# Keys rotated by relative position, context sums beside the query projection, and the two batches' softmax taken apart, in a six-part perceiver kernel

## The chip, the cores and the metric

One Trainium2 chip, one of its cores. The metric is the device time of one execution in microseconds, from the kernel's runs on the chip; the kernel before has a median of 547.14 us over 3 runs.

## What is computed

x (2 x 128 x 256) goes through six residual parts, each behind a layer norm: cross-attention with compressed keys, a state-space layer, a feed-forward, a second cross-attention with quantised operands, an attention over the batch axis, and a gated feed-forward. The change lies in the first one. Its core, in the reference:

```python
kv_c = kv @ W_kvc                       # 2 x 2048 x 64
q_c = q @ W_dq                          # 2 x 128 x 96
q_rope = _rope(q_rope, lq)              # position of the query, 64 columns a head
k_rope = _rope(kv_c @ W_kr, lk)         # position of the key, shared by the heads
scores = (q_nope @ k_nope + q_rope @ k_rope) * scale      # einsum, 16 heads
good = (k_ids <= qs) & (k_ids >= qs - 8)                  # qs: a segment id for each query
scores = jnp.where(good[:, None, :, :], scores, NEG)
out = softmax(scores) @ v                                 # then @ W_o
```

A query sees at most nine keys, those from its segment id less 8 up to the id. If it sees none, softmax over equal values gives the mean of all 2048 values of its batch. The kernel takes that case along as a tenth kind of key, for which it needs the mean of the context over its rows.

## The kernel before

The program is written out by hand for each engine, with counting semaphores between them; each engine works through its list in order, so a wait holds back whatever stands behind it. TensorE's results go to eight PSUM banks of 128 x 512 words (`ps`).

First part, in the order of TensorE's list:

- L1342, L1344: the key up-projection is folded into the query's (`w_qall`, 64 latent and 64 rotated columns a head), and W_kr into `w_kcat`. Then the layer norm's transposes (L1335) and the projection to 96 latents (L1351).
- The query loop, over 8 pairs of heads: L1375 gives 128 rows for each head, 64 latent and 64 to be rotated, for 256 queries; L1377 gives the 64 rotated rows once more with their halves exchanged (`w_qrs`, made by ACT at L714). ACT copies the latent rows to `qT` (L738), DVE multiplies the rows of L1375 by cosines and those of L1377 by sines (L1010, L1012), GpSimd adds both into `qT` (L601). Each output has two banks. From the fourth pair on, `window_columns(0, f)` (L1363, ACT L732) transposes the gathered context rows of batch 0 in between, five groups.
- The nine context rows of each query and nine rows of a table of cosines and sines (`rope`, by the key's position) come by GpSimd's indirect loads (L589, L592), at indices that DVE works out (L974 to L979).
- Keys: L1395 projects the gathered rows with `w_kcat`, three steps a batch, with `window_columns(1, f)` between the batches. ACT copies 64 latent columns to `krow` (L750); DVE rotates the other 64 (L1025 to L1030). SP stores the latents of each batch to DRAM (L506) and, when both are there, loads them back grouped by eight queries in nine loads (L510) to `kvg`, where they serve as values.
- L1404 transposes `krow` to `kcat` in six steps, with ACT L755. L1438 makes the scores, 32 groups of eight queries times 16 heads against 72 keys, four groups a step, and DVE adds the mask (L1034). Both batches' scores stand together, with the products of W_uv and W_o (`weights_vo`, L1413) between.
- Softmax for each batch: maximum (L1045), subtraction (L1046), exponential on ACT (L759), sum (L1039 or L1054), reciprocal (L1040 or L1055), product (L1056).
- Context sums: SP loads the context in eight chunks of 512 rows through two buffers (L494), GpSimd adds four chunks a batch into `csums` of 128 x 4 x 256 (L612), and TensorE sums over partitions and the four tiles with a column of ones (`mean_column`, L1422, 16 matmul records a batch). The mean goes through `w_kcat` (L1453) to `kvm`, copied by ACT for batch 0 (L775) and DVE for batch 1 (L1059), and by a small load (L516) to row 73 of `kvg`.
- L1462 transposes the probabilities in eight steps (ACT L778), L1474 multiplies them with `kvg` in four (DVE L1063 to `oT`), L1479 gives the output, both batches in one bank, DVE adds it to the residual (L1066), and `normalise(1)` follows (L956 to L966).

SP's list before: chunks 0 and 1 (once the rotation rows are there), w0b (W_uv and W_o), chunk 2, store of batch 0, chunk 3, chunk 4, store of batch 1, chunk 5, the nine loads, chunks 6 and 7, w1 (the next part's weights), the small load. GpSimd's list: the gathers, eight additions of the query loop, then the chunks.

An fp32 matmul leaves two matmul records in the trace (a transpose one), so a pair of heads in the loop shows four of L1375 and four of L1377.

## Time and profile before

| | |
|---|---|
| median of 3 runs (lowest, highest) | 547.14 us (542.32, 548.55) |
| the profiled execution | 546.76 us |
| its span, first to last instruction | 544.9 us |
| TensorE matmuls busy | 437.3 us (80%) |
| DVE busy | 398.5 us (73%) |
| ACT busy | 296.0 us (54%) |
| GpSimd busy | 138.8 us (25%) |
| chain that ended last | PE 54%, DVE 17%, issue 14%, ACT 8%, DMA 3% |

The busy shares are means over parts with different limits: the second cross-attention, from about 230 to 480 us, is full on TensorE, DVE and ACT, while the first part has DVE at about a half. So the shares say little of the changed part, and the views of its own stretch are what count. The chain of waits is followed back from the last instruction; in time order it shows at each moment whose work set the end.

### The profile page before, as it was taken

Reading aid. Unit: us, or ns where it says so; the run is one execution under the profiler, and the core shown is the slowest. Engines: PE = TensorE matmul, PEld = TensorE weight load, DVE = VectorE, ACT = ScalarE, POOL = GpSimd, SP = SyncE. Lnnn points to the kernel's source line nnn. Section 1 sums busy time; section 2 is a strip of 40 time slices with the busy share of each in tenths; the row PEclk is TensorE's granted clock in tenths of the full one; section 3 lists DMA queues with packets and bytes.
Section 4 is the critical chain, followed back from the end, with each engine's and each line's share of the span. In section 5 each row is a group of like instructions: output and inputs, shape, how many; then the busy total and the mean of one; then the engine's idle time right before and its main releaser. Section 6 shows DMA issues by size and latency. Waiting matters only on the chain.

```text
span 544.9 us, 9508 instructions
## 1 busy us (share of the span) xinstructions
PE 437.3 (80%) x3874; PEld 328.4 (60%) x3914; DVE 398.5 (73%) x607; ACT 296.0 (54%) x384; POOL 138.8 (25%) x176
## 2 busy tenths in 40 slices
PE   3999887788488777767866789899898988876597
PEld 3556776666265555533753567677677767654486
DVE  6134585357969999995669899999999999613242
ACT  2123424045454444431437899999999999931110
POOL 4124441013545555550001233242111111100000
PEclk9999996989699999989889799999999999977789
DMA  8820692131122111004519545544455334000000
GB/s 300 344 91 0 195 246 100 37 158 36 43 95 80 60 58 58 2 0 169 217 47 396 203 159 229 226 165 156 174 228 219 157 156 156 2 1 0 1 1 19
DMA packets 14822, 67.94 MB, mean 125 GB/s; under 512 B 6154, under 2 KB 8762, under 8 KB 11706
## 3 DMA queue, kind: packets, MB, share of 16 engines
q1 hardware_dynamic: 14202, 63.78, 31.8%
q0 software_dynamic: 576, 3.54, 1.7%
q8 instruction: 31, 0.51, 0.4%
q14 instruction: 13, 0.11, 0.1%
HBM read 66.16 MB, written 1.15 MB: 124 GB/s over the span
## 4 chain that ended last, share of the span: by engine, by line
PE 54%; DVE 17%; issue 14%; ACT 8%; DMA 3%; POOL 2%; SPq 1%; DVEq 0%; ACTq 0%; POOLq 0%
PE ps L1705 10%; PE ps L1684 6%; PE ps L1718 4%; PE ps L1793 3%; ACT arena L915 3%; PE ps L1717 3%; DVE arena L1138 3%; DVE arena L1147 3%; PE ps L1375 2%; PE ps L1377 2%; PE ps L1395 2%; DVE arena L1100 2%; PE ps L1505 2%; PE ps L1626 2%; PE ps L1573 2%
## 5 line engine op out<-in xcount | busy, mean ns | idle before, releaser
L1245 DVE CUSTOM_DVE_ANT_0 arena<-ps,arena 128x1024 f32<-128x1024 f32 x88 | 109.1, 1279 | 3.7 <-PE ps L1684 3.6
L1705 PE MATMUL ps<-cst,arena 128*128 128x128 f32 x512 | 78.8, 277 | 18.5 <-ACT arena L915 16.8
L1705 PEld LDWEIGHTS ps<-cst,arena 128*128 128x128 f32 x512 | 61.1, 141 | 50.9 <-ACT arena L906 32.5
L906 ACT ACTIVATE arena<-arena 128x4096 uint8<-128x4096 f32 x22 | 81.7, 3714 | 7.1 <-POOL arena L682 7.0
L1684 PE MATMUL ps<-arena 128*128 128x512 bf16 x216 | 68.5, 383 | 8.0 <-DVE arena L1245 3.4
L1718 PE MATMUL ps<-vrow,arena 128*128 128x16 f16 x1024 | 60.5, 169 | 0.0
L1718 PEld LDWEIGHTS ps<-vrow,arena 128*128 128x128 f16 x1024 | 54.1, 97 | 1.4
L1245 DVE CUSTOM_DVE_ANT_0 w<-ps,arena 128x1024 f32<-128x1024 f32 x40 | 50.0, 1279 | 3.6 <-PE ps L1684 2.7
L915 ACT ACTIVATE arena<-ps 128x512 f32<-128x512 f32 x96 | 50.0, 586 | 1.6 <-PE ps L1718 1.5
L1717 PE MATMUL ps<-vrow,arena 128*128 128x16 f16 x768 | 49.9, 170 | 0.0
L649 POOL TENSOR_TENSOR arena<-arena 128x1024 f32<-128x1024 f32 x16 | 37.5, 2366 | 47.6 <-DVE arena L1138 47.3
L678 POOL TENSOR_SCALAR arena<-arena 128x1 f32<-128x1 f32 x32 | 11.7, 366 | 144.2 <-DVE arena L1245 144.2
L1717 PEld LDWEIGHTS ps<-vrow,arena 128*128 128x128 f16 x768 | 47.2, 96 | 0.0
L906 ACT ACTIVATE arena<-w,arena 128x4096 uint8<-128x4096 f32 x10 | 37.1, 3713 | 5.3 <-POOL arena L682 5.3
L833 ACT ACTIVATE arena<-arena 128x254 f32<-128x254 f32 x64 | 27.0, 495 | 18.8 <-DVE arena L1138 18.8
L1138 DVE TENSOR_TENSOR_SCAN arena<-arena 128x1024 f32<-128x1024 f32 x16 | 35.7, 2273 | 0.0
L583 POOL TENSOR_TENSOR ln_rs<-ln_ve,neghalf 128x2 f32<-128x2 f32 x6 | 4.2, 706 | 103.3 <-DVE ln_ve L963 103.3
L1522 PE MATMUL ps<-w,arena 128*128 128x256 f32 x128 | 30.3, 379 | 0.0
L1529 PE MATMUL ps<-arena,w 128*128 128x512 f32 x64 | 28.8, 592 | 0.0
L704 ACT ACTIVATE xnT<-ps 128x512 f32<-128x512 f32 x6 | 3.6, 598 | 44.1 <-PE ps L1335 44.1
L1522 PEld LDWEIGHTS ps<-w,arena 128*128 128x128 f32 x128 | 24.3, 190 | 3.9
L1254 DVE TENSOR_SCALAR arena<-ps 128x1024 f16<-128x1024 f16 x32 | 22.0, 686 | 5.9 <-PE ps L1718 5.9
(266 smaller groups left out, 818.3 us busy)
## 6 DMA issues: line engine op xcount, KB each, us to landing
arena<-ks_scr SPq DMA_DIRECT2D x16, 2048.0 KB, 8.1
arena<-in_context SPq DMA_DIRECT2D x16, 512.0 KB, 3.4
arena<-in_w SPq DMA_DIRECT2D x1, 4488.0 KB, 13.5
w<-in_w SPq DMA_DIRECT2D x1, 2927.0 KB, 13.6
arena<-in_w0b SPq DMA_DIRECT2D x1, 2560.0 KB, 11.2
arena<-in_w SPq DMA_DIRECT2D x1, 2048.0 KB, 8.3
arena<-bc_scr SPq DMA_DIRECT2D x16, 128.0 KB, 3.5
arena<-in_fill SPq DMA_DIRECT2D x1, 2048.0 KB, 7.0
```

Of the source, the lines that this page charges most:

```text
L649: pool.tensor_tensor(dbx[:, s], u[:, :, :], bcb[:, n % 4, :].unsqueeze(1).broadcast_to([P, ET, T]), ALU.mult)\
L833: ins = act.activation(dA[:, s, t, :].rearrange("p (b l) -> p b l", b=B)[:, :, 1:L], delta[:, t, :].rearrange("p (b l) -> p b l", b=B)[:, ...
L906: act.activation(out8[:, :, 0], s_sb[u % 3], ACT.Exp, bias=nb[:, u % 3:u % 3 + 1], accum_out=zall[:, u:u + 1]).then_inc(p_ready, 1)
L915: act.activation(ptr[:, c, :].bitcast(F32), bank(4 + n % 3, 0, 512), ACT.Copy).then_inc(ptr_sb[1], 1)
L1138: dve.tensor_tensor_scan(hst[:, s, :], dA[:, s].rearrange("p t n -> p (t n)"), dbx[:, s].rearrange("p t n -> p (t n)"), 0.0, ALU.mult, ALU ...
L1245: dve.tensor_tensor_reduce(s_sb[slot][:, keys], ps[:, 2 * (c % 2):2 * (c % 2) + 2, :].rearrange("p a n -> p (a n)"), ksb[h % 2][:, keys], ...
L1522: mm = pe.matmul(bank(2 + a, t * D, D), cT[:, c, k:k + P], w_kv[:, c, 0:D], start=False, stop=(c == CH - 1), skip_group_check=True)
L1529: mm = pe.matmul(bank(m, 0, CK), w_kv[:, c, D + m * P:D + (m + 1) * P], cT[:, c, :], start=(c == 0), stop=(c == CH - 1))
L1684: mm = pe.matmul(bank(2 * (c % 2) + m, 0, 512), qz[h // 8][:, h % 8, b * L:(b + 1) * L], kT[:, h // 8, k:k + 512], start=True, stop=True)
L1705: mm = pe.transpose(bank(4 + n % 3, k * P, P), words[:, w:w + P], ident)
L1717: pe.matmul(bank(7, u * HW, HW), neg1024[:, :], vrow[:, h // 2, v:v + HW], start=False, stop=False)
L1718: mm = pe.matmul(bank(7, u * HW, HW), ptr[:, c, k * 2 * P + par:(k + 1) * 2 * P:2], vrow[:, h // 2, v:v + HW], start=(t == 0), stop=(t == ...
```

## The change

- **Rotation.** The score of a rotated query at position i and a rotated key at position j depends on j - i alone. So queries aren't rotated at all, and the gathered key rows, which belong to one query each, are rotated by j - i. The table begins at position -127, and the row index gets 127 less the partition (`back`). `w_qrs`, L1377, the two DVE multiplies, GpSimd's addition and ACT's copy go; one DVE copy per pair takes all 128 rows to `qT`. The loop uses four banks.
- **Context sums.** SP issues chunks 2 to 5 ahead of the store of batch 0, chunks 6 and 7 ahead of that of batch 1. GpSimd begins the additions right behind the gathers, and folds the four tiles of each batch to one by two more additions; `mean_column` has two matmuls a batch instead of eight.
- **Softmax taken apart.** TensorE's list now goes: keys of batch 0, windows of batch 1, transposes of batch 0, keys of batch 1, scores of batch 0, transposes of batch 1, two vo products, scores of batch 1, two more, column sums, probabilities 0 and 1, mean latents, probabilities 2 and 3, latents 0 and 1, probabilities 4 and 5, output of batch 0, probabilities 6 and 7, latents 2 and 3, output of batch 1. The outputs have a bank for each batch, and DVE adds and takes the statistics batch by batch. DVE does the probabilities of batch 0 ahead of the last two score evictions. The copies to `kvm` and `oT` are ACT's, and ACT's second exponential stands behind four copies of probabilities.

```diff
@@ -69,7 +69,7 @@
 def adds(c):
 
     per = NC // B
-    return c // per * (per - 1) + max(c % per, 1)
+    return c // per * (per + 1) + max(c % per, 1)
...
@@ -500,17 +497,21 @@
             chunk(1)
             sp.dma_start(w0b[:, :], w0b_d).then_inc(ld_w0b, 16)
 
-            for b in range(B):
-                chunk(2 * b + 2)
+            def key_rows(b):
+
                 sp.wait_ge(kc_sb, 3 * b + 3)
                 sp.dma_start(kv_scr[b * L:(b + 1) * L, :, :], krow[:, b, :, 0:KVC]).then_inc(st_kv, 16)
-                chunk(2 * b + 3)
+
+            for c in range(2, 6):
+                chunk(c)
+            key_rows(0)
+            chunk(6)
+            chunk(7)
+            key_rows(1)
             sp.wait_ge(st_kv, 32)
             for j in range(WIN):
                 sp.dma_start(kvg[j * GQ:(j + 1) * GQ, :, :], kv_scr[:, j, :].rearrange("(g i) k -> i g k", i=GQ))\
...
-            for p in range(PAIRS):
-                pool.wait_ge(rq_ready, p + 1)
-                r = rq[R:2 * R, p % 2]
-                pool.tensor_tensor(qT[R:2 * R, :, 2 * p:2 * p + 2, :], r[:, 0].rearrange("p o (g i) -> p g o i", i=GQ),
-                                   r[:, 1].rearrange("p o (g i) -> p g o i", i=GQ), ALU.add).then_inc(qr_sb, 1)
-            pool.wait_ge(qr_sb, PAIRS)
...
+                if k == NC // B - 1:
+                    for n in (2, 1):
+                        pool.wait_ge(csum, adds(c) + 2 - n)
+                        pool.tensor_tensor(csums[:, b, 0:n], csums[:, b, 0:n], csums[:, b, n:2 * n], ALU.add).then_inc(csum, 1)
...
-            for k in range(2):
-                act.activation(w_qrs[0:QC, :, k * half:(k + 1) * half], w_qr[0:QC, :, (1 - k) * half:(2 - k) * half], ACT.Copy)\
-                   .then_inc(wq_made, 1)
...
-            for p in range(PAIRS):
-                act.wait_ge(qpair, p + 1)
-                act.activation(qT[0:KVC, :, 2 * p:2 * p + 2, :],
-                               bank(p % 2, 0, 512, 0, KVC).rearrange("p (o g i) -> p g o i", o=2, i=GQ),
-                               ACT.Copy).then_inc(qa_sb, 1)
-                if p >= 3:
-                    window_columns(0, p - 3)
...
+            key_rows(0)
+            for f in range(5):
+                window_columns(1, f)
+            key_cat(0)
+            key_rows(1)
+            key_cat(1)
             exponentials(0)
             for n in range(4):
...
+            act.wait_ge(pe_step, MTR)
+            act.activation(mT[:, :], bank(7, 8, B * CH), ACT.Copy, scale=1.0 / NKEY).then_inc(mtr_sb, 1)
+
...
+            for n in range(2):
+                prob_columns(n)
+            act.wait_ge(pe_step, MLAT)
+            for b in range(B):
+                act.activation(kvm[:, b * GB:(b + 1) * GB, :], bank(7 - b, 64 * (1 - b), KVC, 0, 1).unsqueeze(1)
+                               .broadcast_to([1, GB, KVC]), ACT.Copy).then_inc(kvm_ready, 1)
+            for n in range(2, 4):
+                prob_columns(n)
+            exponentials(1)
+            latent_columns(0)
+            latent_columns(1)
+            for n in range(4, 8):
+                prob_columns(n)
+            latent_columns(2)
+            latent_columns(3)
 
 
...
             for b in range(B):
                 ins = dve.tensor_scalar(idx[:, b:b + 1], base[:, b:b + 1], float(b * NKEY), None, ALU.add)
...
                 dve.wait_ge(qpair, p + 1)
-                four = [R, 2, B, L]
-                cosb = qcos[R:2 * R, :].unsqueeze(1).unsqueeze(1).broadcast_to(four)
...
-                split = "p (o b l) -> p o b l"
-                dve.tensor_tensor(r[:, 0].rearrange("p o (b l) -> p o b l", b=B),
-                                  bank(p % 2, 0, 512, R, R).rearrange(split, o=2, b=B), cosb, ALU.mult)
-                dve.tensor_tensor(r[:, 1].rearrange("p o (b l) -> p o b l", b=B),
-                                  bank(2 + p % 2, 0, 512, R, R).rearrange(split, o=2, b=B), sinb, ALU.mult).then_inc(rq_ready, 1)
+                dve.tensor_copy(qT[:, :, 2 * p:2 * p + 2, :], bank(p % 4, 0, 512).rearrange("p (o g i) -> p g o i", o=2, i=GQ))\
+                   .then_inc(qa_sb, 1)
 
             for n in range(6):
...
+                if n == 3:
+                    largest_scores(0)
                 if n == 5:
...
+                    probabilities_of(0)
+            largest_scores(1)
+            probabilities_of(1)
...
-            dve.wait_ge(pe_step, MLAT)
-            dve.tensor_copy(kvm[:, GB:2 * GB, :], bank(6, 0, KVC, 0, 1).unsqueeze(1).broadcast_to([1, GB, KVC]))\
-               .then_inc(kvm_ready, 1)
-            for n in range(4):
-                dve.wait_ge(pv0, n + 1)
-                dve.tensor_copy(oT.rearrange("k p (g i) -> k g p i", i=GQ)[:, 8 * n:8 * n + 8],
-                                bank(4 + n % 2, 0, 512).rearrange("k (g p i) -> k g p i", g=8, p=PAIRS)).then_inc(ot_sb, 1)
-            dve.wait_ge(pe_step, MLA_OUT)
-            dve.tensor_tensor(xres[:, :, :], bank(0, 0, 512).rearrange("p (b d) -> p b d", b=B), xres[:, :, :], ALU.add)\
-               .then_inc(mla_done, 1)
-            dve.wait_ge(mla_done, 1)
-
-
-            normalise(1)
+                    link(ins)
...
+            normalise(1, attended)
...
             for p in range(PAIRS):
-                if p >= 2:
-                    pe.wait_ge(qa_sb, p - 1)
-                    pe.wait_ge(rq_ready, p - 1)
+                if p >= 4:
+                    pe.wait_ge(qa_sb, p - 3)
                 for o in range(2):
-                    pe.matmul(bank(p % 2, o * T, T), w_qall[0:QC, 2 * p + o, :], q_cT[0:QC, :], start=True, stop=True)
-                for o in range(2):
-                    mm = pe.matmul(bank(2 + p % 2, o * T, T, R, R), w_qrs[0:QC, 2 * p + o, :], q_cT[0:QC, :],
-                                   start=True, stop=True)
+                    mm = pe.matmul(bank(p % 4, o * T, T), w_qall[0:QC, 2 * p + o, :], q_cT[0:QC, :], start=True, stop=True)
                 mm.then_inc(qpair, 1)
                 if p >= 3:
                     window_columns(0, p - 3)
...
 
-                pe.wait_ge(csum, adds((b + 1) * NC // B - 1))
+                pe.wait_ge(csum, (b + 1) * (NC // B + 1))
                 for c in range(CH):
-                    for t in range(CT):
-                        mm = pe.matmul(bank(7, 8 + CH * b + c, 1), csums[:, b, t, c * P:(c + 1) * P], ones[:, 0:1],
-                                       start=(t == 0), stop=(t == CT - 1))
+                    mm = pe.matmul(bank(7, 8 + CH * b + c, 1), csums[:, b, 0, c * P:(c + 1) * P], ones[:, 0:1], start=True, stop=True)
                 return mm
...
+                    mm = pe.matmul(bank(b, 0, D), oT[:, p, b * L:(b + 1) * L], w_vo[:, p, :],
                                    start=(p == 0), stop=(p == PAIRS - 1))
+                mm.then_inc(mla_out, 1)
+
+            project_keys(0)
+            for f in range(5):
+                window_columns(1, f)
+            pe.wait_ge(qa_sb, PAIRS)
+            turned_keys(0)
+            project_keys(1)
+            scores_of(0)
+            turned_keys(1)
+            pe.wait_ge(ld_w0b, 16)
+            weights_vo(0)
+            weights_vo(1)
+            scores_of(1)
+            pe.wait_ge(kr_ps, 6)
+            weights_vo(2)
+            weights_vo(3)
+            mean_column(0)
+            mean_column(1).then_inc(pe_step, 1)
+            prob_columns(0)
+            prob_columns(1)
+            pe.wait_ge(mtr_sb, 1)
+            pe.wait_ge(wvo_sb, 4)
+            for b in range(B):
+                for c in range(CH):
+                    mm = pe.matmul(bank(7 - b, 64 * (1 - b), KVC, 0, 1), mT[:, CH * b + c:CH * b + c + 1], w_kcat[:, c, 0:KVC],
+                                   start=(c == 0), stop=(c == CH - 1))
             mm.then_inc(pe_step, 1)
+            prob_columns(2)
+            prob_columns(3)
+            pe.wait_ge(ld_kvg, 16 * (WIN + 1))
+            weighted_latents(0)
+            weighted_latents(1)
+            prob_columns(4)
+            prob_columns(5)
+            attended(0)
+            prob_columns(6)
+            prob_columns(7)
+            weighted_latents(2)
+            weighted_latents(3)
+            attended(1)
...
     cst[:, 0:128] = np.eye(P)
-    cst[R:, 128:256] = rope[:L, 0:R].T
-    cst[R:, 256:384] = rope[:L, R:].T
+    cst[:, 128] = L - 1 - np.arange(P)
```

## Rows read from the trace of the kernel before

**Rows 1.** The chain of waits in order: start us, us, what, with records.
```profile
19.86 2.08 PE ps L1375 x4
21.94 1.90 PE ps L1377 x4
...
35.55 1.05 PE ps L1363 x4
...
47.07 1.01 PE ps L1377 x4
...
51.48 4.48 PE ps L1395 x36
...
59.41 4.48 PE ps L1395 x36
...
64.27 2.89 DMA kv_scr<-arena
...
84.16 3.57 PE ps L1422 x16
...
105.87 0.70 DVE xres L1066
...
111.39 7.03 PE ps L1505 x24
```

**Rows 2.** The records of line 1375: nanoseconds min/median/max, first and last start.
```profile
L1375 PE MATMUL ps<-arena x32: 378/634/797, 19.9 to 49.1; 96*128 96x256 f32 x32
```

**Rows 3.** Stretches: length, busy (x) by engine, granted clock, DMA share, GB/s.
```profile
19.86:45.90 26.04, 26.04 (x61) 14.15 (x62) 7.51 (x12) 4.74 (x8) 6.37 (x5) 1.00 0.36 142
...
84.00:87.50 3.50, 3.35 (x16) 3.35 (x16) 3.43 (x4) 0.00 (x0) 0.10 (x1) 0.50 0.39 167
...
112.00:114.00 2.00, 2.00 (x6) 0.50 0.90 377
...
93.00:93.25 0.25, 1.00 0.12 27
```

**Rows 4.** Groups by line, 19 to 110 us: busy us, mean ns | idle before.
```profile
L1438 PE MATMUL ps<-arena 128*128 128x72 f32 x64 | 7.5, 275 | 0.2 <-DVE arena L1034 0.2
...
L1479 PE MATMUL ps<-arena 128*128 128x256 f32 x32 | 7.2, 382 | 0.0
...
L1474 PE MATMUL ps<-arena 73*64 73x64 f32 x128 | 4.1, 223 | 0.0
...
L1413 PE MATMUL ps<-arena 128*64 128x256 f32 x32 | 3.9, 385 | 0.0
...
L1063 DVE COPY arena<-ps 128x512 f32<-128x512 f32 x4 | 2.8, 692 | 5.0 <-PE ps L1474 5.0
...
L1404 PE MATMUL ps<-cst,arena 128*128 128x128 f32 x18 | 2.6, 279 | 0.6 <-ACT arena L755 0.6
```

**Rows 5.** Instructions in order of time, 59 to 92 us: start, us, what.
```profile
72.43 1.38 DVE L1046 TENSOR_TENSOR arena<-arena 128x1168 f32<-128x1168 f32 x1
...
73.83 1.18 ACT L759 ACTIVATE arena<-arena 128x1168 f32<-128x1168 f32 x1 [6.34 <-DVE arena L1046]
...
77.41 1.37 DVE L1045 TENSOR_REDUCE arena<-arena 128x16 f32<-128x1168 f32 x1
...
78.81 3.08 DVE L1046 TENSOR_TENSOR arena<-arena 128x1168 f32<-128x1168 f32 x1
...
90.53 1.01 ACT L775 ACTIVATE arena<-ps 1x1024 f32<-1x1024 f32 x1 [0.35 <-PE ps L1453]
...
91.77 0.61 SPq L516 DMA_DIRECT2D arena<-arena  x1
```

**Rows 6.** DMA issues, 0 to 130 us: KB each, median us to landing.
```profile
arena<-in_context SPq DMA_DIRECT2D x9, 512.0 KB, 3.8
w<-in_w SPq DMA_DIRECT2D x1, 2927.0 KB, 13.6
arena<-in_w0b SPq DMA_DIRECT2D x1, 2560.0 KB, 11.2
```

## What was predicted, before the kernel was changed on the chip

> **What bounds the kernel now.** I read the chain of waits in order of time first, because it says which work sets the end and where the changed part lies in it. The first layer's cross-attention is all that the diff touches, and it runs from the start to the addition to the residual at 105.87 us [rows 1]. No line behind it is changed, so what that stage gains or loses arrives at the end as a shift. Inside the stage the chain is almost only TensorE: the query projections from 19.86 to 51.48, the key projection of batch 0 to 55.96, which I call T, and then another 50 us. The one long departure from TensorE begins at 64.27, with a store of the key rows; behind it on SP's queue come nine gathers and a context chunk, then two GpSimd additions, and only at 84.16 the column sums of batch 1 [rows 1]. TensorE sat idle for the last 4.1 us of that.
>
> Next I looked at how fast TensorE went. The median record of a 96x256 projection takes 634 ns and the shortest 378 [rows 2]; in the chain four L1377 records cost 1.90 us at first and 1.01 from 47 us on [rows 1]. That is the step from 1.2 to 2.4 GHz, although the granted clock stands as 1.00 for the whole stretch [rows 3]: the record holds no change before about 46 us, so I read the pace and not that column. TensorE was busy for all 26.04 us of it [rows 3].
>
> **The query loop.** Eight times, once per pair of heads, it issues two L1375 matmuls (four records) and two L1377 matmuls with the half-swapped weights (four records). The change deletes the L1377 half: in the chain six times 1.90 and twice about 1.0, together 13.4 us [rows 1]. DVE's two multiplies, GpSimd's addition and ACT's 64x512 copy go too; one DVE copy of 128x512 takes their place, for which L1063 has 692 ns [rows 4]. TensorE needs 2.0 us (slow) or 1.0 us (fast) per pair and has four banks to run ahead into, so the copy costs nothing; without the banks it would cost 0.7 us a pair, 5.6 us in all. The two weight copies that ACT loses lay ahead of a wait for TensorE and give nothing. The new row index of the rotation table is one small DVE instruction in place of another, and fetches as many bytes.
>
> What remains is eight pairs and five transpose groups: at the slow pace 8 x 2.0 + 5 x 1.05 = 21.3 us, to 41.1; at the fast one 8 x 1.0 + 5 x 0.55 = 10.8 [rows 1]. So the gain depends on when the clock rises, and the trace gives bounds. Late: at the same moment, 45.9. Then the key projection of batch 0 (4.48 us fast, some 9.0 slow) begins at 41.1, does 4.8 of its 9.0 slowly and the rest in 2.1: T = 48.0, 8.0 us earlier. Early: after the layer norm TensorE starts 128-row work at 111.39, at 0.50, and goes at the full clock about 3.5 us later [rows 1, 3]. Had the loop that too, it would do 1.75 pairs in its first 3.5 us and the rest in 6.25 x 1.0 + 5 x 0.55 = 9.0: T = 19.9 + 3.5 + 9.0 + 4.5 = 36.9, 19.1 us earlier. Between the ends I take the late one, because the nearest rows are the loop's own: 26 us without a gap did not lift the clock, and the last few us before it rose hold no denser work than those before them.
>
> The Trainium skill ("TensorE: Matmul & The Clock Gate", Part 1) says that the array goes to its full clock after a short time of sustained busyness. By that rule the loop would be fast almost from its start, and the time would be that of rival 1 below; the trace does not agree, as TensorE was busy all through 19.86 to 45.90 at the slow pace.
>
> **After T, step by step, at full clock.** Times are T plus so much; the terms are rows of before.
> - Window columns of batch 1 as before, 3.4 us; three transposing steps, now ahead of the second projection, 1.2; the projection 4.5 [rows 1, 4]: T + 9.1.
> - Scores of batch 0, 4 x 0.9 (64 records, eight a step [rows 4]), with 0.3 for DVE, which finishes the last rotation first: T + 13.0.
> - Three transposing steps 1.6, two vo products 1.95, scores 3.6, two more products 1.95 [rows 4], and both batches' column sums, now 4 records each and not 16 (3.57 at half clock [rows 1]), 1.0 together: T + 23.1. Beside this DVE and ACT do the softmax of batch 0: maximum 1.37, subtraction 1.38, exponential 1.18, sum and product 1.37 and 1.38 [rows 5], evictions between. It is over 0.6 us before it is wanted. A GpSimd addition beside it makes 1.38 into 3.08 [rows 5]; with the cover gone that is about 1.5 us.
> - Transposed probabilities 2 x 0.7 (four transposes a step, L1404 has three), mean latents 1.0, again 1.4: T + 26.9. **A new wait** stands here: both kvm copies are now ACT's, 1.01 each [rows 5], where DVE and ACT did them side by side. They end at T + 27.6, and the small load behind them moved its bytes within 1.7 us of its issue [rows 3, 5]: T + 29.3. TensorE idles 2.4 us. Queued on ACT behind the kvm copies are two probability copies and the exponentials of batch 1.
> - Two latent steps 2.0 [rows 4]: T + 31.3. **A second wait**: ACT reaches the exponentials at T + 28.8, and DVE needs 3.0 behind them: the probabilities of batch 1 come at T + 33.1, after 1.8 us of idleness.
> - Transposes 1.4, output of batch 0 3.6 (half of L1479), transposes 1.4, latents 2.0, one ACT copy 0.7, output of batch 1 3.6 [rows 4]: T + 45.8.
> - Half the addition, and one bn_stats where two stood, since batch 0's lie under TensorE: T + 46.6. Before, that point was at T + 51.4. Gain 4.8 us.
>
> **The sums.** GpSimd is free of the rotations and starts on chunk 1 at about 24. The chunk loads stand ahead of the stores on SP. Chunks 2 and 3 come behind w0b, which needs 11.2 us from 21.0; each later round is 3.8 us of load [rows 6] and 2.35 of addition. SP is held by the first key-row store until T + 0.4, and chunks 6 and 7 wait behind it; they are added by about 58, and the two new folding additions, half and quarter as long, end near 60. TensorE asks at T + 22, which is 70. So the 4.1 us of idleness and the stretch at 0.50 behind it [rows 3] go; they are in the 4.8. The nine gathers start at T + 12 and are issued by T + 17. Only w1 behind them, 13.6 us with a megabyte ahead of it now [rows 6], may keep the small kvm load back, by up to 1.7 us; by bytes it needs 10.1 and just gets out of the way, so I take zero and keep 1.7.
>
> **Sum.** 8.0 + 4.8 = 12.8 us off the profiled execution's 546.76 gives 534.0. The median shown, 547.14, is 0.4 above it: 534.4, and I say 534.5.
>
> **The rivals.**
> 1. The clock rises early: T = 36.9, the gain is 19.1 + 4.8 = 23.9, about 523. For it: the loop loses its 64-column half and is denser. Against it: the unbroken slow 26 us [rows 3]. The rule of the Trainium skill named above would give this one.
> 2. The clock rises as long after the first window transposes as before (35.5 to 45.9 [rows 1], 10.4 us). They now come at 27.9, so it rises at 38.3: the loop ends near 39.7, T = 44.2, the gain is 11.8 + 4.8 = 16.6, about 530.5. For it: the rise did follow them. Against it: they are 1.05 us in 4.65.
> 3. The two new waits let the clock fall, as 4.1 us of idleness did [rows 3]. Some 7 us of the tail at half speed add 3.5 and w1 adds 1.7: about 539.5. Against it: the waits are shorter, and work lies between them.
> 4. Slower than before: the rise hangs on how much of the loop's work has passed, so that with the L1377 matmuls gone the slow pace reaches far into the softmax. Each further microsecond of slow TensorE work costs 0.5, so a rise after about 72 us uses up the whole gain; at 85 it would be about 553. Against it: dense work that began at 0.50, at 84 and at 111 us, found the full clock within some microseconds, and the key projections are dense.
>
> That the column sums come last, as now, would need them 10 us later than I reckon; I count it with rival 3.
>
> **How the numbers follow.** The forecast (531 to 538) gets 0.51, rival 1 0.20, rival 2 0.17, rival 3 0.08, rival 4 0.04. The range takes in rival 1 with 2 us beyond it, and above the forecast the w1 and contention bounds and rival 3: 521 to 540. A measurement of this kernel can tell about 1% from no change, which is 5.5 us, or 541.7. Faster 0.92, same 0.04, slower 0.04.
>
> **What the profile would show.** No L1377 records, eight pairs of four records each. T near 48; near 37 or 44 it is rival 1 or 2, and the change of pace in the 96x256 records gives the moment. No idle TensorE ahead of the column sums; two idle spells of 2.4 and 1.8 us, before the latents, released by the kvm load, and before the fifth step of probabilities, released by DVE. The addition ends about T + 46. I would be wrong if the granted clock shows 0.50 between T + 26 and T + 46, if GpSimd or SP again stand in the chain, or if DVE's copies hold back the loop.

## The result and the profile after

| | before | after |
|---|---|---|
| median of 4 runs (lowest, highest) | 547.80 us (542.32, 548.55) | 528.80 us (526.91, 530.82) |
| ratio, with its 95% interval | | 0.9675 [0.9601, 0.9748] |
| the profiled execution; its span | 546.76; 544.9 us | 528.54; 526.7 us |
| T, the end of the first key projection | 55.96 | 36.94 |
| last bn_stats of the stage | 107.36 = T + 51.4 | 86.64 = T + 49.7 |
| from there to the end of the span | 437.5 us | 440.1 us |

The kernel became faster by about 18 to 19 us (547.14 or 547.80 less 528.80), where 12.6 were forecast. The profiled executions differ by 18.2 us, and the table splits them: T came 19.0 us earlier, what follows T in the stage became 1.7 us shorter, and what lies behind the stage took 2.5 us longer. The direction and the range held. The first term was 11 us too small, the second 3.1 us too large, and the third had been taken as nothing.

The chain of waits of the changed kernel, in the columns of [rows 1]: start, us, what.

```profile
20.88 5.66 PE ps L1384 x16
26.54 0.44 PE ps L1373 x4
26.98 0.87 PE ps L1384 x4
...
32.45 4.49 PE ps L1398 x36
...
58.53 0.98 PE ps L1440 x8
...
62.97 5.16 DMA arena<-arena
68.16 3.69 PE ps L1461 x64
71.85 1.91 PE ps L1449 x8
73.76 4.64 PE ps L1468 x16
...
79.28 2.04 PE ps L1461 x64
...
81.99 3.73 PE ps L1468 x16
```

L1384 is the query projection, which was L1375 and L1377. Its first 16 records take 5.66 us, and from 26.98 on four take 0.87, where four of L1375 took 2.08 and four of L1377 1.90 before [rows 1]. The store of the key rows, and the wait for the column sums behind it, are gone from the chain: the sums (L1440) stand between other TensorE work. A small DMA of 5.16 us is new in it. Behind it the latents (L1461) take 3.69 us for 64 records, and 2.04 for the next 64: the slow and the fast pace. The records of L1384, in the columns of [rows 2]:

```profile
L1384 PE MATMUL ps<-arena x32: 377/379/796, 20.9 to 31.4; 96*128 96x256 f32 x32
```

The median is 379 ns, where it was 634 [rows 2]: most of the loop ran at 2.4 GHz. Around the DMA, and behind the stage, the stretches in the columns of [rows 3] read:

```profile
62.00:68.16 6.16, 0.01 (x1) 0.00 (x0) 3.00 (x3) 2.96 (x5) 0.00 (x0) 0.81 0.79 336
68.16:72.00 3.84, 3.84 (x65) 3.72 (x66) 0.00 (x0) 0.70 (x2) 0.00 (x0) 0.50 0.02 4
72.00:78.00 6.00, 6.00 (x23) 5.29 (x23) 0.00 (x0) 1.68 (x3) 0.00 (x0) 0.66 0.00 0
...
90.70:99.00 8.30, 8.26 (x25) 6.55 (x26) 3.49 (x8) 3.02 (x6) 0.39 (x1) 0.65 0.34 143
```

TensorE did nothing for 6.15 us while the DMA engines moved 336 GB/s. The granted clock fell while it idled, it came back at 0.50, which is 1.2 GHz, and was at full clock only some way into the output of batch 0.

### The profile page after: what moved, and what is told of

The parts are those of the page before. It is cut to its first block, busy times and chain, and to the rows that moved or that the text cites. A ratio compares the mean times of both kernels' runs of the same rounds, so it can differ in the third digit from the quotient of the medians.

```text
span 526.7 us, 9396 instructions
## 1 busy us (share of the span) xinstructions
PE 424.1 (81%) x3858; PEld 322.3 (61%) x3858; DVE 387.6 (74%) x595; ACT 293.7 (56%) x379; POOL 132.8 (25%) x172
## 4 chain that ended last, share of the span: by engine, by line
PE 56%; DVE 18%; issue 13%; ACT 9%; DMA 2%; POOL 1%; SPq 0%; DVEq 0%; ACTq 0%; POOLq 0%
PE ps L1734 11%; PE ps L1713 7%; PE ps L1747 4%; PE ps L1822 4%; ACT arena L933 3%; PE ps L1746 3%; DVE arena L1148 3%; DVE arena L1157 3%; PE ps L1534 2%; PE ps L1384 2%; PE ps L1655 2%; DVE arena L1110 2%; PE ps L1398 2%; PE ps L1602 2%; PE ps L1468 2%
## 5 line engine op out<-in xcount | busy, mean ns | idle before, releaser
L1713 PE MATMUL ps<-arena 128*128 128x512 bf16 x256 | 77.3, 383 | 4.3 <-DVE arena L1255 3.5
L1551 PE MATMUL ps<-w,arena 128*128 128x256 f32 x128 | 32.0, 395 | 0.0
L1551 PEld LDWEIGHTS ps<-w,arena 128*128 128x128 f32 x128 | 25.8, 202 | 4.6
```

Source lines behind the costliest of these rows:

```text
L1551: mm = pe.matmul(bank(2 + a, t * D, D), cT[:, c, k:k + P], w_kv[:, c, 0:D], start=False, stop=(c == CH - 1), skip_group_check=True)
L1713: mm = pe.matmul(bank(2 * (c % 2) + m, 0, 512), qz[h // 8][:, h % 8, b * L:(b + 1) * L], kT[:, h // 8, k:k + 512], start=True, stop=True)
```

## The experiments

In all of them "stage" is the time from T to the end of the last addition to the residual, and "rest" is from there to the end of the span. The first weights landed at different moments from run to run, in the kernels whose start is the same too, so the first layer's first projection begins anywhere between 9.1 and 11.2 us and shifts everything behind it. I therefore compare stretches, each read from one profiled execution, and totals only with their intervals. Each ratio is to runs of the kernel before from the same occasion, and the median of those was not the same each time: 547.80 us for `after`, 547.59 for e1 to e4, 545.08 for e5 to e8, 547.05 for e9 to e11 and 544.76 for e12. So medians of different occasions can't be compared to within some 3 us, and the ratios are the fairer measure there. "One run" has no interval.

| | median us | ratio to before | first projection | T | stage | rest |
|---|---|---|---|---|---|---|
| before | | | 9.10 | 55.96 | 50.6 | 438.3 |
| after | 528.80 | 0.9675 [0.9601, 0.9748] | 10.11 | 36.94 | 49.3 | 440.5 |
| e1_rot_only | 532.38 | 0.9711 [0.9645, 0.9778] | 10.38 | 38.72 | 50.9 | 440.6 |
| e2_before_wide | 537.31 | 0.9808 [0.9757, 0.9859] | 10.74 | 45.00 | 53.0 | 440.1 |
| e3_after_half | 546.18 | one run | 9.68 | 54.28 | 49.8 | 440.2 |
| e4_after_wide | 537.38 | one run | 10.33 | 44.99 | 50.0 | 440.6 |
| e5_w1_behind | 525.05 | 0.9644 [0.9583, 0.9704] | 9.17 | 36.18 | 46.8 | 439.7 |
| e6_kvm_two | 526.79 | 0.9656 [0.9583, 0.9729] | 11.17 | 38.05 | 45.6 | 441.9 |
| e7_warm | 529.67 | 0.9721 [0.9664, 0.9778] | 10.89 | 37.22 | 50.0 | 440.0 |
| e8_warm_w1_kvm | 524.51 | 0.9628 [0.9571, 0.9686] | 10.53 | 34.65 | 47.6 | 440.3 |
| e9_w0b_behind | 526.37 | 0.9602 [0.9575, 0.9630] | 10.19 | 37.89 | 46.6 | 440.9 |
| e10_warm_longer | 524.13 | 0.9572 [0.9519, 0.9625] | 10.86 | 33.61 | 50.3 | 439.8 |
| e11_all | 526.75 | 0.9619 [0.9588, 0.9650] | 11.11 | 34.89 | 49.8 | 440.0 |
| e12_early_chunks | 521.86 | 0.9626 [0.9532, 0.9721] | 10.63 | 33.38 | 46.8 | 439.7 |

### What kept the clock down in the query loop

The theory was that the 64-column matmuls of L1377 held the slow pace, so that taking them out lifted the clock early. The rivals were that the amount of work decides, or the moment of the window transposes. Four kernels tell them apart.

**e1_rot_only** is the kernel before with the rotation change alone: the loop of `after` with its four banks, and SP's order, the sums and the softmax of `before`.

```diff
-            dve.tensor_copy(idx[:, B:2 * B], base[:, :])
+            dve.tensor_scalar(idx[:, B:2 * B], base[:, :], back, None, ALU.add)
...
-                if p >= 2:
-                    pe.wait_ge(qa_sb, p - 1)
-                    pe.wait_ge(rq_ready, p - 1)
+                if p >= 4:
+                    pe.wait_ge(qa_sb, p - 3)
```

> The kernel before with the rotation alone changed: queries not rotated, keys by relative position, the loop with 4 banks; the lists of SP, the context sums and the softmax stay. Theory A (the query loop carries nearly all of the gain, because the clock rises early once the 64-column matmuls are out of it): the 96x256 records turn from about 0.63 to 0.38 us within 5 us of the first, T (end of the first key projection) near 37, but the column sums still come last, as SP loads the last chunks behind the nine gathers: about 545 less 19, some 3 us above the changed kernel, 529 to 533. Theory B (the early rise comes from GpSimd's additions or SP's order and not from the loop): T near 44 to 48 and 535 to 540.

Its loop, from the first query record to the first key-projection record, takes 13.1 us (21.15 to 34.24), where it was 31.6 before and 11.6 after. That gives 532.38 us, 3.6 above the changed kernel, and the intervals of the two ratios overlap. Of the 3.5 us between the two profiled executions 1.5 lie in the loop, where the clock rose later than in `after` (the first 16 query records took 7.17 us, and 5.66 there); only 1.6 lie in the stage, and that is what the other parts of the change are seen to be worth. Its stage is as long as before, and its chain shows why:

```profile
47.02 3.55 DMA kv_scr<-arena
...
54.76 5.76 DMA arena<-in_context
...
60.59 2.36 POOL vrow L605
...
63.08 3.30 POOL vrow L605
...
66.43 3.57 PE ps L1393 x16
```

The store of key rows, a chunk, two additions and the column sums follow each other exactly as in [rows 1]: this wait only moved forward with T, and it is the new order of sums and queue that takes it away in `after`.

**e2_before_wide** leaves the kernel before as it is and gives L1377 128 columns of weights. The half swap of the rotation is lost with it, so the queries are rotated wrongly; the work around it is the same.

```diff
-                    mm = pe.matmul(bank(2 + p % 2, o * T, T, R, R), w_qrs[0:QC, 2 * p + o, :], q_cT[0:QC, :],
+                    mm = pe.matmul(bank(2 + p % 2, o * T, T), w_qall[0:QC, 2 * p + o, :], q_cT[0:QC, :],
```

> The kernel before with each 64-column matmul of the query loop (L1377) widened to the 128 columns of L1375: as many matmuls, more of the array used, the same order and waits. (The sine products then take unswapped rows, so the rotation of the queries is wrong.) Theory A (the 64-column matmuls keep TensorE at 1.2 GHz): the pace doubles within 5 us of the first loop record and the kernel gets faster by 8 to 11 us, 536 to 539, with more work. Theory B (the clock rises at some time of its own, or only with fewer matmuls): the pace changes near 46 us as before and the time stays within 2 us of before, 545 to 549.

Every matmul has at least as much work as before, and the kernel is 10 us faster (537.31 against 547.59 on that occasion). Its query records:

```profile
L1375 PE MATMUL ps<-arena x32: 377/379/796, 21.5 to 38.3; 96*128 96x256 f32 x32
...
L1377 PE MATMUL ps<-arena x32: 379/379/634, 23.4 to 39.2; 96*128 96x256 f32 x32
```

The loop takes 19.0 us instead of 31.6. From 26.57 on its chain has 0.86 us for four records.

**e3_after_half** and **e4_after_wide** start from the changed kernel and put two unused matmuls per pair back, into a free bank: with 64 columns, as L1377 had, or with 128.

```diff
                     mm = pe.matmul(bank(p % 4, o * T, T), w_qall[0:QC, 2 * p + o, :], q_cT[0:QC, :], start=True, stop=True)
+                for o in range(2):
+                    pe.matmul(bank(6, o * T, T, R, R), w_qall[0:QC, 2 * p + o, KVC:2 * KVC], q_cT[0:QC, :], start=True, stop=True)
```

> The changed kernel with two 64-column matmuls per pair of heads put back into TensorE's list, their result unused; nothing on the other engines comes back. Theory A (64 columns keep the clock low): slow pace to about 45 us, T near 55, time 543 to 547. Theory B (the other engines' load or time itself decides): the pace doubles near 25 us, the loop lasts about 8 x 1.0 us longer than in the changed kernel, T near 45, time 536 to 538.

> The changed kernel with two more 128-column matmuls per pair, their result unused: as many matmuls as before, none with 64 columns. Theory A: the pace doubles near 25 us, T near 45, 536 to 538. Theory B (the number of matmuls in the loop decides): slow pace to about 45, T near 55, 543 to 548.

The records of e3_after_half:

```profile
L1384 PE MATMUL ps<-arena x32: 377/634/796, 20.5 to 47.6; 96*128 96x256 f32 x32
...
L1387 PE MATMUL ps<-arena x32: 379/631/689, 22.5 to 48.6; 96*64 96x256 f32 x32
```

Three pieces of its chain:

```profile
22.53 1.90 PE ps L1387 x4
...
41.84 1.18 PE ps L1384 x4
43.02 1.01 PE ps L1387 x4
```

And the records of e4_after_wide:

```profile
L1384 PE MATMUL ps<-arena x32: 377/379/796, 21.1 to 38.6; 96*128 96x256 f32 x32
...
L1387 PE MATMUL ps<-arena x32: 379/379/634, 23.0 to 39.4; 96*128 96x256 f32 x32
```

With 64 columns the loop takes 29.3 us and stays slow up to about 42; with 128 columns, the same number of matmuls and more work in each, 19.4 us. So the gain is not that half the matmuls are gone: with 128-column ones added, twice as many cost 19.4 - 11.6 = 7.8 us. The other 10 us are the pace. TensorE was without a gap in both loops. The rival that the amount of work done sets the rise falls: e3 and e4 issue as many matmuls, those of a pair have a third more columns in e4, and its pace rises about 6 us into the loop where that of e3 rises after about 22. The rival that the window transposes bring it falls too: in e4 and e2 the pace is full before 28 us, and the first transposes are at 31.14 and 30.89. e3 and e4 were run once each; their records and the two medians of e1 and e2 say the same.

Two things stay open. The added 64-column matmuls differ from the wide ones in more than their width: they write to partitions 64 to 127 alone, and they alternate with wider ones. No run has them at another place or by themselves, so what it is in them that held the pace is not shown. Nor is it shown why the pace rose in the end, in the kernel before and in e3, while they still ran.

The Trainium skill ("TensorE: Matmul & The Clock Gate", Part 1) says that a short time of sustained matmul activity lifts the clock. The changed kernel, e1, e2 and e4 agree, with a rise some 4 to 7 us into the loop; the kernel before and e3 do not, with about 26 and 22 us of unbroken slow work. The measurement decides here: the rule was right for the loop that was left, and not for the one I read it against.

### The small load behind the large one

**e5_w1_behind** moves the 2927 KB load of w1 behind the small load that repeats the mean latents to the partitions. **e6_kvm_two** adds to that the kvm copies side by side again, one on ACT and one on DVE.

```diff
-            sp.dma_start(w1[:, :], w1_d).then_inc(ld_w1, 16)
...
+            sp.dma_start(w1[:, :], w1_d).then_inc(ld_w1, 16)
```

```diff
-            for b in range(B):
-                act.activation(kvm[:, b * GB:(b + 1) * GB, :], bank(7 - b, 64 * (1 - b), KVC, 0, 1).unsqueeze(1)
-                               .broadcast_to([1, GB, KVC]), ACT.Copy).then_inc(kvm_ready, 1)
+            act.activation(kvm[:, 0:GB, :], bank(7, 64, KVC, 0, 1).unsqueeze(1)
+                           .broadcast_to([1, GB, KVC]), ACT.Copy).then_inc(kvm_ready, 1)
...
+            dve.wait_ge(pe_step, MLAT)
+            dve.tensor_copy(kvm[:, GB:2 * GB, :], bank(6, 0, KVC, 0, 1).unsqueeze(1).broadcast_to([1, GB, KVC]))\
+               .then_inc(kvm_ready, 1)
```

> The changed kernel with SP's last two loads exchanged: the small kvm load first, w1 behind it. Theory C (the small load waited in the DMA queues behind w1, and the 6.15 us of idle TensorE before the latents comes from that): it lands within 2 us of its issue, the idle time shrinks to some 2.4 us, a second wait of 1 to 2 us for DVE's probabilities appears, the granted clock falls less, and the time drops by 3 to 6 us against the changed kernel, to 523 to 526. Theory D (the kvm path itself, ACT's two copies and the load's own latency, makes the wait): less than 1 us of difference, 528 to 530.

> As e5_w1_behind, and the kvm copies by ACT and DVE side by side as in the kernel before. Theory (ACT's second copy lies on the path to the latents and to the exponentials of batch 1): 1.0 us less ahead of each, 0.5 to 1.5 us faster than e5. Rival (DVE's copy of 1.2 us stands ahead of its own softmax, and the exponentials wait for other things): within 0.5 us of e5.

The chain of e5_w1_behind:

```profile
63.81 1.90 DMA arena<-arena
...
65.75 3.68 PE ps L1461 x64
69.44 1.91 PE ps L1449 x8
71.35 3.87 PE ps L1468 x16
```

The latents in its timeline, with TensorE's idle time ahead of them in brackets:

```profile
65.75 3.68 PE L1461 MATMUL ps<-arena 73*64 73x64 f32 x64 [2.89 <-DMA arena<-arena]
```

The same load takes 1.90 us instead of 5.16, and idleness falls from 6.15 to 2.89 us: 3.3 us of the wait were the bytes of w1 that went first. The load landed at T + 29.5, only 1.7 us earlier after T than in `after`, because it was also issued 1.6 us later (T + 27.6). TensorE began the column sums at T + 23.2 instead of T + 21.6, as a key rotation and a subtraction on DVE, which stood beside GpSimd's additions and took 0.95 and 2.67 us in `after`, took longer here and are on the chain:

```profile
43.46 2.06 DVE L1042 TENSOR_TENSOR arena<-arena 128x192 f32<-128x192 f32 x1
...
51.86 3.21 DVE L1049 TENSOR_TENSOR arena<-arena 128x1168 f32<-128x1168 f32 x1
```

The output of batch 1 ended at T + 46.4. The clock still fell, so even 2.89 us of idleness, with sparse work ahead of it, left the 64 latents at 3.68 us. The stage shrank by 2.5 us, the median by 3.7; the intervals of the two ratios overlap.

In e6 the load landed at T + 28.0 and the output ended at T + 45.2, 1.2 us better than e5. Its total is no better, and the table shows why it can't tell: the first projection began 2.0 us later, and T came 1.9 us later. The stage is the evidence, 45.6 against 46.8.

### The start, and what is late once it is quicker

**e7_warm** adds nine unused fp32 matmuls of 128x128x256 at the very start, so that the clock may already be up. **e8_warm_w1_kvm** is e6 with them. **e10_warm_longer** is e5 with 17 of them. **e9_w0b_behind** is e5 with the w0b load behind chunks 2 and 3, to bring the additions out from between the key rotations, and **e11_all** is e9 with the 17 matmuls. **e12_early_chunks** is e10 without SP's wait for the rope gather ahead of the first chunk.

```diff
+            pe.wait_ge(warm_set, 1)
+            for _ in range(9):
+                pe.matmul(bank(6, 0, T), warm[:, 0:P], warm[:, P:P + T], start=True, stop=True)
```

> The changed kernel with nine fp32 matmuls of 128x128 by 256 columns on a constant tile, unused, while the first weights load (TensorE idles there to about 10 us). Theory A (128-column work lifts the clock, 64-column work doesn't, wherever it stands): full clock before the first real matmul; L1352 takes 2.7 us and not 5.35, the first projections 1.5 us less, the query loop is fast from its first record and saves 1.9: 5 to 7 us in all, 522 to 524. Rival (the rise depends on time since the start, or the 64-column L1342 work at about 10 us lets the clock fall again): the loop still begins slowly, 527 to 531.

> e6 and e7 together. If the two gains lie in different stretches they add: 517 to 520. If the earlier start only makes the sums or the loads come last (POOL L606 or DMA in the chain of waits), no better than the better of the two, 522 to 525.

```diff
-            sp.dma_start(w0b[:, :], w0b_d).then_inc(ld_w0b, 16)
...
-            for c in range(2, 6):
-                chunk(c)
+            chunk(2)
+            chunk(3)
+            sp.dma_start(w0b[:, :], w0b_d).then_inc(ld_w0b, 16)
+            chunk(4)
+            chunk(5)
```

> e5 with the w0b load behind chunks 2 and 3 on SP's queue instead of ahead of them: w0b is wanted only after the first scores, near 51 us. Theory (chunks 2 and 3 wait in the DMA queues for w0b): they land 3 to 4 us earlier, the column sums of batch 0 are folded before the first key rotation, and the rotations and subtractions of DVE run less beside GpSimd's additions: 0 to 2 us faster than e5, 523 to 525. Rival: chunk 2 and w0b now pass DMA later, and batch 1's additions fall on the rotations of batch 1 as before: within 0.5 us of e5, or 1 us slower.

> e5 with 17 unused matmuls of 128x128 by 256 columns at the start, where e7 had 9: in e7 the clock had risen at 5 us, the matmuls were over at 7.2, TensorE idled to 10.9 and the clock fell. Now they reach to 10 or 11 us. Theory A: no idle stretch, L1352 in 2.7 us instead of 4.7 to 5.35, the query loop fast from its first record: 5 to 6 us off e5, 519 to 521, unless DVE and GpSimd then are late. Rival (the 64-column matmuls of L1352 and the short gaps to 21 us let the clock fall): the loop begins slowly again, 523 to 527.

> e9 and e10 together. With a fast loop the context sums are the next to come last (in e8 the chain of waits went through the chunk loads and GpSimd's additions to 59.2 us), and the earlier chunks of e9 should take them off: 517 to 520. If the sums still come last: the time of e10.

The timeline of e7_warm, TensorE alone, then a stretch of it in the columns of [rows 3]:

```profile
1.30 5.88 PE L1354 MATMUL ps<-arena 128*128 128x256 f32 x18 [1.30 <-DVE arena L972]
10.89 4.68 PE L1358 MATMUL ps<-arena 128*96 128x64 f32 x32 [3.71 <-DMA arena<-in_w0a]
```

```profile
13.00:24.00 11.00, 9.66 (x36) 7.46 (x35) 1.54 (x3) 2.72 (x6) 1.46 (x1) 0.50 0.77 304
```

The same two instructions in the timeline of e10_warm_longer:

```profile
1.30 9.30 PE L1354 MATMUL ps<-arena 128*128 128x256 f32 x34 [1.30 <-DVE arena L972]
10.86 2.90 PE L1358 MATMUL ps<-arena 128*96 128x64 f32 x32 [0.26 <-DMA arena<-in_w0a]
```

Nine matmuls are over at 7.2, the weights land 3.7 us later, and the granted clock is 0.50 from 13 to 24 us: the first projection is 0.7 us shorter than in `after` (5.35), and the loop is as slow at its start. Seventeen reach to the landing, and the first projection takes 2.90 us instead of 4.68. The loop then began fast, though the clock fell for some 3 us in it, and T came at 33.6, 2.6 us earlier than in e5. Whether the total followed can't be told: the medians differ by 0.9 us, the ratios by 0.7%, and the intervals of the ratios overlap. In the profiles most of it was lost again: the stage of e10 is 3.5 us longer than that of e5, and its chain names most of the cause:

```profile
11.94 10.38 DMA arena<-in_rope,arena
...
22.77 4.25 DMA arena<-in_context
...
27.19 2.36 POOL vrow L608
...
58.32 0.74 POOL vrow L612
...
59.10 0.79 PE ps L1446 x4
```

The column sums come last again. SP waits for a gather of the rope table, then loads the chunks; the folding ends at 59.05, and TensorE waited 2.9 us for it. In e8 too the sums were last. e9 and e11 kept SP's wait and moved the w0b load, and neither can be told from e5 and e10: the intervals of the ratios overlap, and the stages are 46.6 against 46.8 and 49.8 against 50.3. In e11 the sums are off the chain all the same. Its chain has these two pieces:

```profile
44.70 2.15 DVE arena L1047
...
47.27 3.69 PE ps L1430 x16
```

A key rotation beside a GpSimd addition took 2.15 us instead of 0.36 and left TensorE idle for 1.95 us, the granted clock was 0.50 from 47 to 53 us, and half the scores of batch 0 took 3.69 us where it took 2.00 in `after`. TensorE reached the sums only at T + 26.0. So two things are in the way once T is early, the late start of the additions and their place beside DVE's work. e12 moves the start.

```diff
-            sp.wait_ge(got_rope[1], 16)
```

> e10 without SP's wait for the gathered rotation rows ahead of chunk 0: chunks 0 and 1 and w0b are issued once L1360 is done (near 14 us) instead of at 22.4. Theory (in e10 the context sums set the end: GpSimd's first addition began at 27.2 because its chunk was issued so late, and the column sums came 3 us after TensorE wanted them): the first addition begins at 22 to 24, the sums are folded by 55, and the kernel is 2 to 4 us faster than e10, 520 to 522. Rival: the chunks now share the DMA engines with the gathers and hold them back, the window columns wait, and the time stays that of e10 within 1 us.

GpSimd's first addition in e10_warm_longer and in e12_early_chunks, each from its timeline:

```profile
27.19 2.35 POOL L608 TENSOR_TENSOR vrow<-arena 128x1024 f32<-128x1024 f32 x1 [12.75 <-DMA arena<-in_context]
```

```profile
24.11 2.35 POOL L607 TENSOR_TENSOR vrow<-arena 128x1024 f32<-128x1024 f32 x1 [9.70 <-DMA arena<-in_context]
```

The additions start 3.1 us earlier, the folding ends at 54.3 where it ended at 59.05, and the sums are off the chain. The stage is back at 46.8 with T at 33.4, so in the profiled executions e12 is the shortest of all. The totals don't confirm it: its median of 521.86 us is the lowest, but the kernel before was quick on that occasion too (544.76), its ratio of 0.9626 is above that of e9, e10 and e11, and its interval holds most of theirs. One of its four runs was at 528.18. That e12 beats e10 or the changed kernel is likely from the stage, and not shown in the time of the whole.

## Why the prediction was right in its direction, and what failed in it

**The query loop: the mechanism was in the range and the choice between its ends failed.** The step that failed is "Between the ends I take the late one, because the nearest rows are the loop's own". Those rows held the 64-column matmuls that the change removes, so they were not rows of the loop that would be left. e2, e3 and e4 show that these matmuls kept the pace slow. With 128 columns in all of them the pace was full 4 to 7 us into the loop. That the measured time still fell within the range owes to rival 1, which the range took in.

Rival 1 is what happened: T was forecast at 36.9 by it and came at 36.94, and a match that close is luck. Its own working took 3.5 us of slow pace; the chain shows 5.66 us for the first 16 records, against 3.5 at the full clock, with the rise about 4 us in. A pair then took 0.87 us where 1.0 was reckoned, and the loop 11.6 where the working has 12.5. The key projection took 4.49 us as reckoned. The first weights landed 1 us later than in the profile before, so the loop itself gave 20.0 us and not 19.1. The late end was mis-sized too: it took 2.0 us for a slow pair, which is the pace of L1375 next to L1377. Among wide matmuls alone four slow records took 1.71 us (e4):

```profile
24.88 1.71 PE ps L1384 x4
```

**The removed parts and the copy cost what was said.** DVE's copy (L1024) takes 0.69 us and holds nobody; four banks cover it. The steps up to the latents ran a little ahead of the forecast: keys of batch 1 at T + 8.7 (forecast 9.1), scores of batch 0 at T + 12.6 (13.0), column sums at T + 22.5 (23.1), the second pair of probability steps behind the mean latents at T + 25.1 (26.9). The GpSimd addition beside DVE was priced at 1.5 us with its cover gone. L1049 took 2.67 us and not 1.38, and was still covered.

**The kvm load was mis-sized.** Forecast: 1.7 us of transfer and at most 1.7 of delay through w1, taken as zero. Measured: 5.16 us from issue, and e5 shows that 3.3 of them are w1. The byte count gave w1 10.1 us and had it issued at T + 17, so that it would be out of the way at T + 27.1, ahead of the small load at T + 27.6. The 10.1 us were not far off. What failed was the two moments: w1 was issued at 55.82, which is T + 18.9, and the small load at 62.97, which is T + 26.0, 1.9 us later and 1.6 us earlier than reckoned:

```profile
55.82 0.79 SPq L515 DMA_DIRECT2D w<-in_w  x1
```

By the same count w1 is done at 65.9. Packets still ran at 398 GB/s between 65 and 66 us and at 585 between 63 and 64 (length, granted clock, DMA share, GB/s; a share above 1 shows that a figure for one such microsecond is rough):

```profile
63.00:64.00 1.00, 1.00 1.36 585
...
65.00:66.00 1.00, 0.90 0.93 398
```

The wait was 6.15 us where 2.4 were said.

**Rival 3 came true in part, together with rival 1.** The idleness brought the clock down, and its price can be read: latents 3.69 instead of 2.04 us and output of batch 0 4.64 instead of 3.73, by the same work later at the full clock, and transposes 1.91 instead of the 1.4 of the forecast, together 3.1 us. In the other direction the second wait, forecast at 1.8 us, did not appear: the probabilities of batch 1 were ready at 68.07, just before the load landed. The first wait covered it. The sum is then nearly that of the measurement: +1.9 for the landing (T + 31.2 instead of 29.3), +3.1 for the pace, -1.8 for the hidden wait: 3.2, against 3.1 measured between T + 46.6 and T + 49.7.

**The slack of the sums.** They were to end near 60 and be wanted at 70. They ended at 56.1 and were wanted at 58.5: 2.4 us of slack, not 10. My slack was reckoned with the late T; every microsecond that T comes earlier is taken from it. e8 and e10, with T at 34.7 and 33.6, used it up.

**Behind the stage** I had taken a pure shift. The profile before has 438.3 us there, all twelve experiments and the changed kernel 439.7 to 441.9. The nearest rows differ in pace: the first projection behind the layer norm took 7.03 us [rows 1] and now takes 8.27, the granted clock of that stretch being 0.65, and a group of 128 records averages 395 ns (L1551) where it had 379:

```profile
L1551 PE MATMUL ps<-w,arena 128*128 128x256 f32 x128 | 32.0, 395 | 0.0
```

But e2, the old kernel with one line widened, and e3, whose stage ends at 104.0, within 3 us of the old place, have 440.1 and 440.2 too. So neither the new order nor the earlier end is shown to be the cause. The profile before is one execution, runs of that kernel lie between 541.66 and 549.30 us, and whether this stretch was merely quick in it stays open.

**The point.** 528.8 lies 5.7 us below the 534.5 that I gave: 11.0 from T, less 3.1 from the stage and 2.5 from the rest, and 0.3 between the profiled executions and the medians. The three errors partly cancelled.

## What to carry to other kernels

When a trace shows a slow pace, ask which instructions were in that stretch before using it as a bound for what remains: if the change takes out one kind of them, the stretch is no longer the nearest row. A small load on which everything waits must be issued ahead of a large one that nobody wants yet. And a slack that was worked out against one arrival must be worked out again for every rival in which that arrival moves, because a gain ahead of a join stops paying where the other arm takes over.

## What the runs showed of the hardware that was not expected

- **Narrow weights and the clock.** A loop of fp32 matmuls over 96 rows, half of them with 128 columns and half with 64, kept TensorE at 1.2 GHz (634 ns a record) for about 26 us without a gap, and 22 us in e3. With all of them at 128 columns the records fell to 379 ns within 4 to 7 us. Widening a matmul made it cheaper: the e2 loop has more work and is 12.6 us shorter.
- **A short warm-up is lost.** After 5.88 us of unused matmuls and 3.7 us of idleness the granted clock fell within the first real matmuls and was 0.50 from 13 to 24 us (e7). Those that reached to the first real matmul, within 0.26 us, made it 2.90 us and not 4.68 (e10).
- **DVE behind GpSimd.** A DVE instruction of 128x192 with both inputs in SBUF takes 0.36 us alone and up to 2.15 beside one of GpSimd's 2.35 us additions. In e12 three instructions show it:

```profile
31.28 4.85 POOL L607 TENSOR_TENSOR vrow<-vrow,arena 128x1024 f32<-128x1024 f32 x2 [4.82 <-DMA arena<-in_context]
...
31.69 2.15 DVE L1044 TENSOR_TENSOR arena<-arena 128x192 f32<-128x192 f32 x1
33.77 0.34 DVE L1039 TENSOR_TENSOR arena<-ps,arena 128x192 f32<-128x192 f32 x1
```

GpSimd has two additions from 31.28 on. DVE's L1044 begins beside the first and ends at 33.84, as that one ends (31.28 and half of 4.85 is 33.7), while L1039, with one input in PSUM, takes 0.34 us beside the second. The Trainium skill ("SBUF — State Buffer", the section on its two separate sides) says that a DVE instruction with two SBUF inputs and a GpSimd one take a shared pair of ports by turns, each for its whole length; these rows agree.
